# A transformer layer on one core: a two-half buffer for the sums of the values, and ranks counted in one work array

## The chip, the cores and the metric

The kernel runs on one core of a Trainium2 chip. The metric is the device time of one execution in microseconds (us). A core has five engines that run beside each other and meet at semaphores: PE (TensorE, matrix products), DVE (VectorE), ACT (ScalarE), POOL (GpSimd) and SP (SyncE, which here only issues DMAs).

## The reference

Eight sequences of 1,024 tokens with 256 channels go through one transformer layer. Cut to what matters:

```python
q, k, v = heads(ln(x) @ Wq + bq), heads(ln(x) @ Wk + bk), heads(ln(x) @ Wv + bv)   # 16 heads of 16
attn = softmax(where(causal, q @ k.T * scale, -inf))
x = x + ((attn * gate_of_each_key) @ v) @ Wo + bo
sc = sigmoid(ln(x) @ gate_w.T) + gate_bias           # 8 experts, 4 groups of 2
keep the 2 best groups, in them the 2 best experts (ties: the lower number first)
x = x + sum over the 2 experts of weight * ffn_e(ln(x)) + shared_ffn(ln(x))
```

## The kernel before

A batch is one of the eight sequences `n`. For each batch and each group `g` of four heads the kernel computes the running maxima of the scores (`M` on PE, `MR` on DVE, line 1549), then the scores (`QK` on PE, line 1941), their exponentials (`EX` on ACT, line 1358, into `probs`), the causal mask on the diagonal blocks (`MK` on POOL, line 1175), and the sums of the values (`PV` on PE, line 1961), which add up in one PSUM bank per half `c` of the queries (`CHUNKS` is 2, 512 queries each). When a half is summed, ACT copies the bank to SBUF (`OE`, `copy_o`, line 1369, into `o_sb`) and SP stores it to HBM (`SO`, `store_o`, line 978). That is 64 copies and 64 stores. `o_sb` is one buffer, so each copy waits on the semaphore `o_st` of the store before it, which belongs to the other half.

Behind the attention of batch `n` come its output product, the layer norm, the router's logits and the shared experts, quarter by quarter (`CW`, `CT`, `CG`, `EU`, `HT`, `ED`). The router then picks two experts for each token on DVE (`RO`, the function `routing`): `choose_op` ranks the four groups and then the eight experts with `rank_op`. A rank is the number of rivals that are greater, plus the number of equal rivals with a lower number. `rank_op` counts it in a cube of all pairs (128 partitions x 8 tiles x 8 x 8). For batches 0 to 6 it ranks all eight tiles of a batch at once (`ROUTE`), and the rows are scattered to their experts; for the last batch each quarter ranks its own two tiles (`DENSE_OPS` steps), and all eight experts are computed densely with the weights in `rank`, which line 1816 multiplies in.

No engine's order is written by hand. `plan_work` lists every piece of work with an engine, a planned duration, a due time, what it waits for and which PSUM bank it takes, and `Plan.run` lays them out in time; each engine then runs its pieces in the planned order. `LATER` is a table of offsets to the due times, one per kind of work. A change of one planned duration or one dependency can therefore move any later piece of work on any engine. Where the plan leaves PE idle for 500 ns or more while a sum is open, `keep_busy` puts in matmuls of zeros (line 858).

Of the kernel before, what the change touches and what calls it, by code (L numbers as in the profile page):

```python
# [79 lines left out]
RANK_OP = 13  # L80
# [20 lines left out]
DENSE_OPS = 19  # L101
# [227 lines left out]
def plan_work():  # L329
# [107 lines left out]
    def attention(n, g, s):  # L437
# [17 lines left out]
        if s in LAST_STEP:  # L455
# [3 lines left out]
                [("SO", (u - 1) // (GROUPS * CHUNKS), (u - 1) // CHUNKS % GROUPS, (u - 1) % CHUNKS)] if u else []),  # L459
# [70 lines left out]
    def routing(n):  # L530
        begin = at(n + 1) + T * SHARE_TO - 10000
        for r, step in enumerate(ROUTE[n]):
            ns = 620 if step in range(9, RANK_OP + 1) else 150
# [97 lines left out]
def build(nc, ins, out):  # L631
# [4 lines left out]
    with ExitStack() as ctx:  # L636
# [75 lines left out]
        o_sb = sb("o_sb", [P, CHUNK])  # L712
# [14 lines left out]
        cmp_b = sb("cmp_b", [P, TILES, EXPERTS, EXPERTS])  # L727
# [12 lines left out]
        slot_f = sb("slot_f", [P, 2, TILES])  # L740
        slot_u = sb("slot_u", [P, 4, 2, TILES], mybir.dt.uint32)
        owner, owner_old = sb("owner", [P, SLOT_TILES]), sb("owner_old", [P, SLOT_TILES])
        owner_i = sb("owner_i", [P, 2, SLOT_TILES], mybir.dt.int32)
        share = sb("share", [P, 2, TILES])
# [134 lines left out]
        def _(sp):  # L879
# [95 lines left out]
            def store_o(item, n, g, c):  # L975
                b, k = release["OE", n, g, c]
                sp.wait_ge(freed[b], k)
                sp.dma_start(o_s[bass.ds((n * GROUPS + g) * P, P), c * CHUNK:(c + 1) * CHUNK], o_sb[:]).then_inc(o_st[c], 16)
# [270 lines left out]
        def _(act):  # L1249
# [110 lines left out]
            def copy_o(item, n, g, c):  # L1360
# [104 lines left out]
        def _(dve):  # L1465
# [135 lines left out]
            def rank_op(r, v, n_v, to, ts):  # L1601
                a, b_ = cmp_a[:, ts, 0:n_v, 0:n_v], cmp_b[:, ts, 0:n_v, 0:n_v]
# [8 lines left out]
                if r == 2:  # L1611
                    return nc.vector.tensor_tensor(b_, other, mine, ALU.is_gt)
                if r == 3:
                    return nc.vector.tensor_tensor(a, a, b_, ALU.add)
                return nc.vector.tensor_reduce(to, a, X_AXIS, ALU.add)

            def choose_op(r, ts):
# [9 lines left out]
                if r < 8:  # L1627
                    return rank_op(r - 3, grp[:, ts, :], EXPERTS // 2, rank_g[:, ts, :], ts)
                if r == 8:
# [4 lines left out]
                return rank_op(r - 9, sel[:, ts, :], EXPERTS, rank[:, ts, :], ts)  # L1634
# [15 lines left out]
            def slot_op(n, step):  # L1650
# [58 lines left out]
                return nc.vector.tensor_copy(slot_u[:, n % 4, :, :], slot_f[:])  # L1709

            def owner_op(n, step):
# [10 lines left out]
                if step in ("owner_old", "owner"):  # L1722
                    return nc.vector.tensor_reduce((owner_old if step == "owner_old" else owner)[:], ends, X_AXIS, ALU.add)
                if step == "within":
                    return nc.vector.scalar_tensor_tensor(out=owner_old[:], in0=owner_old[:], scalar=float(EXPERTS),
# [419 lines left out]
```

## Time and profile before

| | |
|---|---|
| median of 3 executions | 1803.69 us (1797.37 to 1806.76) |
| the profiled execution's own time | 1808.59 us |
| its span, first to last instruction | 1806.6 us |
| mean granted TensorE clock | 0.962 of full |
| PE busy | 1653.0 us, 91% |
| DVE busy | 1292.4 us, 72% |
| ACT busy | 1081.9 us, 60% |
| POOL busy | 811.8 us, 45% |

The profile is of one execution, which was 4.9 us above the median. Busy shares are shares of the span. An instruction is named by its line in the kernel, its engine, its operation and output<-inputs.

### The profile page before, as it was taken

The numbers are of one execution on the slowest core, as the hardware profiler recorded it, in microseconds if no ns is written. First come the engines' busy times: TensorE is split into PE (matmuls) and PEld (weight loads), VectorE is DVE, ScalarE is ACT, GpSimd is POOL, SyncE is SP. The second block draws the span as 40 slices with busy tenths as digits, with TensorE's granted clock in tenths as the row PEclk, the third lists the DMA queues.
The fourth block names the chain that finished last, engine by engine and source line by source line (L and its number), as shares of the span: only waits on it lengthen the run. The fifth ranks groups of instructions, "written<-read, shape, count | busy, mean of one in ns | idle before, by whom it ended". The sixth has DMA issues, their size and how long they took to land.

```text
span 1806.6 us, 34673 instructions
## 1 busy us (share of the span) xinstructions
PE 1653.0 (91%) x12785; PEld 982.5 (54%) x12785; DVE 1292.4 (72%) x2528; ACT 1081.9 (60%) x1808; POOL 811.8 (45%) x1390
## 2 busy tenths in 40 slices
PE   7798989989988999899998989999999889999888
PEld 3344446435544566455654555555564557666677
DVE  5776767967795777777785757877688666963655
ACT  3466756665655655675656755586556765568432
POOL 5234533463345221632237863363207773157760
PEclk9699999999998999999998999999999999999999
DMA  5556655554445532644545665453535675336440
GB/s 151 158 156 194 176 169 152 182 153 124 125 127 147 158 104 87 174 113 120 159 118 151 185 194 152 127 162 108 147 93 172 198 197 159 97 129 199 135 122 13
DMA packets 192708, 261.25 MB, mean 145 GB/s; under 512 B 19616, under 2 KB 127264, under 8 KB 192544
## 3 DMA queue, kind: packets, MB, share of 16 engines
q1 hardware_dynamic: 181792, 229.67, 44.0%
q0 software_dynamic: 10752, 29.37, 5.6%
q8 instruction: 105, 1.72, 0.4%
q14 instruction: 59, 0.48, 0.1%
HBM read 130.98 MB, written 127.40 MB: 143 GB/s over the span
## 4 chain that ended last, share of the span: by engine, by line
PE 54%; DVE 14%; DMA 8%; ACT 8%; POOL 8%; issue 5%; SPq 3%; another core or an unknown queue 0%; POOLq 0%; ACTq 0%; DVEq 0%
PE ps_all L1961 10%; PE ps_all L2071 10%; DVE mx L1549 7%; PE ps_all L1941 6%; PE ps_all L1908 6%; PE ps_all L2102 5%; PE ps_all L1892 4%; ACT probs L1358 4%; PE ps_all L1878 3%; PE ps_all L1970 3%; POOL xs_s L1207 2%; PE ps_all L2081 2%; PE ps_all L2034 1%; DMA rr<-r_s 1%; DMA out<-rr 1%
## 5 line engine op out<-in xcount | busy, mean ns | idle before, releaser
L1549 DVE TENSOR_REDUCE mx<-ps_all 128x2 f32<-128x1024 f32 (+2 forms) x640 | 619.0, 1006 | 132.5 <-PE ps_all L1908 74.4
L1358 ACT ACTIVATE probs<-ps_all 128x1024 f32<-128x1024 f32 x576 | 571.8, 1028 | 218.0 <-PE ps_all L1941 209.9
L1175 POOL TENSOR_SCALAR_AFFINE_SELECT probs<-probs 128x256 f32<-128x256 f32 (+1 forms) x448 | 190.9, 443 | 495.5 <-ACT probs L1358 491.3
L1961 PE MATMUL ps_all<-probs,vaug 128*32 128x512 f32 (+3 forms) x3072 | 319.4, 516 | 21.9 <-POOL probs L1175 15.3
L1908 PE MATMUL ps_all<-k_st,q_st 63*128 63x512 f32 (+3 forms) x1536 | 269.3, 401 | 48.0 <-ACT probs L1358 16.3
L1941 PE MATMUL ps_all<-q_st,k_st 64*128 64x512 f32 (+3 forms) x1536 | 265.6, 401 | 29.3 <-ACT probs L1358 9.9
L1908 PEld LDWEIGHTS ps_all<-k_st,q_st 63*128 63x128 f32 x1536 | 135.1, 193 | 163.7 <-issue 52.2
L1941 PEld LDWEIGHTS ps_all<-q_st,k_st 64*128 64x128 f32 x1536 | 130.9, 191 | 158.9 <-issue 67.2
L2071 PE MATMUL ps_all<-w_hi,x2h 128*128 128x512 f32 (+1 forms) x480 | 168.2, 350 | 4.3 <-DVE x2l L1598 2.5
L1804 DVE SCALAR_TENSOR_TENSOR act_t<-act_t,ps_all 128x256 f32<-128x256 f32 x168 | 70.4, 419 | 123.4 <-ACT act_t L1421 110.9
L2071 PE MATMUL ps_all<-w_lo,x2h 128*128 128x512 f32 (+1 forms) x480 | 157.0, 327 | 0.0
L2071 PE MATMUL ps_all<-w_hi,x2l 128*128 128x512 f32 (+1 forms) x480 | 157.0, 327 | 0.0
L1421 ACT ACTIVATE act_t<-ps_all 128x256 f32<-128x256 f32 x168 | 64.6, 385 | 151.3 <-PE ps_all L2071 122.2
L1961 PEld LDWEIGHTS ps_all<-probs,vaug 128*32 128x32 f32 x3072 | 73.2, 110 | 131.6 <-issue 89.4
L1207 POOL DMA_INDIRECT xs_s<-xnb,slot_u x112 | 111.6, 996 | 42.9 <-issue 39.8
L1219 POOL DMA_INDIRECT yab<-ys_s,slot_u x112 | 108.3, 967 | 33.0 <-issue 20.2
L2102 PE MATMUL ps_all<-w_hi,h_hi 128*128 128x256 f32 (+1 forms) x336 | 109.5, 326 | 7.7 <-DVE h_lo L1831 6.9
L2071 PEld LDWEIGHTS ps_all<-w_hi,x2h 128*128 128x128 f32 x480 | 90.8, 189 | 27.6 <-issue 19.7
L1878 PE MATMUL ps_all<-wvd,xt 128*128 128x384 f32 x256 | 96.9, 506 | 1.8 <-issue 0.9
L2071 PEld LDWEIGHTS ps_all<-w_hi,x2l 128*128 128x128 f32 x480 | 90.9, 189 | 8.4
L1831 DVE TENSOR_TENSOR h_lo<-ps_all,h_hi 128x256 fp32r<-128x256 f32 x168 | 70.0, 419 | 35.1 <-ACT h_hi L1436 32.7
L2102 PE MATMUL ps_all<-w_lo,h_hi 128*128 128x256 f32 (+1 forms) x336 | 94.3, 281 | 0.0
(195 smaller groups left out, 2849.8 us busy)
## 6 DMA issues: line engine op xcount, KB each, us to landing
qk_s<-qh SPq DMA_DIRECT2D x116, 256.0 KB
q_st<-qk_s SPq DMA_DIRECT2D x128, 192.0 KB
k_st<-qk_s SPq DMA_DIRECT2D x128, 192.0 KB
xs<-xs_s SPq DMA_DIRECT2D x72, 256.0 KB
ys_s<-ysb SPq DMA_DIRECT2D x72, 256.0 KB
o_s<-o_sb SPq DMA_DIRECT2D x64, 256.0 KB
qk_s<-ql SPq DMA_DIRECT2D x57, 256.0 KB
xs_s<-ysb SPq DMA_DIRECT2D x20, 512.0 KB, 6.0
```

Of the source, the lines that this page charges most:

```text
L1175: last = nc.gpsimd.affine_select(out=block, in_=block, compare_op=ALU.is_ge, fill=0.0, base=0, pattern=[[0, heads], [1, P]], channel_multi ...
L1207: nc.gpsimd.indirect_dma_start(xs_s[i % 2], bass.IndirectOffsetOnAxis(ap=slot_u[:, n % 4, a, t:t + 1], axis=0), xnb[:, t, :], None).then_i ...
L1219: nc.gpsimd.indirect_dma_start(yab[:, t % 2, a, :], None, ys_s[SET_OF[n] % 2], bass.IndirectOffsetOnAxis(ap=slot_u[:, n % 4, a, t:t + 1], ...
L1358: nc.scalar.activation(to, of, ACT.Exp, scale=DH ** -0.5).then_inc(freed[release[item][0]], 1)
L1549: last = nc.vector.tensor_reduce(to[:, :, p, qt % QPC], both[:, :, at:at + keys], X_AXIS, ALU.max)
L1878: last = mm(bank(item)[:, 0:E + DP], xt[:, k, tt * P:(tt + 1) * P], wvd[:, k, :], start=(k == 0), stop=(k == KE - 1))
L1892: last = mm(bank(item), w[:, k, m * P:(m + 1) * P], xt[:, k, :], start=(k == 0), stop=(k == KE - 1))
L1908: last = mm(bank(item, j)[:, to:to + keys], q_st[r, q_half(n, g, c), p, qt % QPC * P:(qt % QPC + 1) * P], k_st[r, k_half(n, g, kc), p, 0:k ...
L1941: last = mm(bank(item, j)[:, to:to + cols], k_st[r, k_half(n, g, kt // QPC), a, kt % QPC * P:(kt % QPC + 1) * P], q_st[r, q_half(n, g, c), ...
L1961: last = mm(bank(first)[32 * h:32 * h + 32, q0 - c * CHUNK:], vaug[:, kt, g, h * VW:h * VW + 32], probs[:, s % 2, h, at:at + cols], start= ...
L2071: last = mm(bank(item)[:, to], x[:, buf, k, t * P:(t + 1) * P], w[:, k, cs], start=(k == 0 and j == 0), stop=(k == KE - 1 and j == 2))
L2102: last = mm(bank(first)[:, t * E:(t + 1) * E], h[:, z % 2, i * P:(i + 1) * P], w[:, cs], start=(item == first and i == 0 and j == 0), stop ...
```

## The change

`o_sb` gets a half for each half of the queries, and the copy of a half waits only for the store of the same half in the group before. In the plan the copy depends on the store two places back instead of one. `rank_op` counts the equal rivals in the work array `cmp_a` and reduces them, then counts the greater ones in the same array, reduces those into a small piece of `cmp_b`, and adds the two results; it had filled two arrays, added them and reduced once. It is six instructions instead of five, and it is called twice in a ranking, so `RANK_OP` and `DENSE_OPS` grow by two. In the plan one more step has the long duration (620) and one more the short one (150) in each ranking of batches 0 to 6. `cmp_b` shrinks from eight tiles to two; `slot_f`, `share` and `owner_old` become views of the work arrays.

```diff
-RANK_OP = 13
+RANK_OP = 15
-DENSE_OPS = 19
+DENSE_OPS = 21
...
             add("ACT", ("OE", n, g, c), 466, due + 4000, [("PV", n, g, s)] + (
-                [("SO", (u - 1) // (GROUPS * CHUNKS), (u - 1) // CHUNKS % GROUPS, (u - 1) % CHUNKS)] if u else []),
+                [("SO", (u - 2) // (GROUPS * CHUNKS), (u - 2) // CHUNKS % GROUPS, c)] if u >= CHUNKS else []),
                 frees=(first, None))
...
-            ns = 620 if step in range(9, RANK_OP + 1) else 150
+            ns = 620 if step in range(10, RANK_OP + 1) else 150
...
-        o_sb = sb("o_sb", [P, CHUNK])
+        o_sb = sb("o_sb", [P, CHUNKS, CHUNK])
...
-        cmp_b = sb("cmp_b", [P, TILES, EXPERTS, EXPERTS])
+        cmp_b = sb("cmp_b", [P, 2, EXPERTS, EXPERTS])
...
-                if c:
-                    act.wait_ge(o_st[0], (gi + 1) * 16)
-                else:
-                    act.wait_ge(o_st[1], gi * 16)
+                if gi:
+                    act.wait_ge(o_st[c], gi * 16)
                 first = FIRST_STEP[c]
-                nc.scalar.copy(o_sb[:], bank(("PV", n, g, first))).then_inc(freed[release[item][0]], 1)
+                nc.scalar.copy(o_sb[:, c, :], bank(("PV", n, g, first))).then_inc(freed[release[item][0]], 1)
...
-                a, b_ = cmp_a[:, ts, 0:n_v, 0:n_v], cmp_b[:, ts, 0:n_v, 0:n_v]
+                a, others = cmp_a[:, ts, 0:n_v, 0:n_v], cmp_b[:, 0, 0:ts.stop - ts.start, 0:n_v]
...
                 if r == 2:
-                    return nc.vector.tensor_tensor(b_, other, mine, ALU.is_gt)
+                    return nc.vector.tensor_reduce(to, a, X_AXIS, ALU.add)
                 if r == 3:
-                    return nc.vector.tensor_tensor(a, a, b_, ALU.add)
-                return nc.vector.tensor_reduce(to, a, X_AXIS, ALU.add)
+                    return nc.vector.tensor_tensor(a, other, mine, ALU.is_gt)
+                if r == 4:
+                    return nc.vector.tensor_reduce(others, a, X_AXIS, ALU.add)
+                return nc.vector.tensor_tensor(to, to, others, ALU.add)
```

The planned order differs in more places than these lines. On PE the orders are the same up to the scores (line 1941) that stand ahead of the place below, in the second batch's attention, and differ from there on: 6,213 rows before, 6,211 now. At that place stood, before:

```order
L1908 MATMUL ps_all<-k_st,q_st 128x512 x2
L1941 MATMUL ps_all<-q_st,k_st 128x512 x2
L858 MATMUL ps_all<-bars,scan 64x512
L1878 MATMUL ps_all<-wvd,xt 128x384 x2
L2102 MATMUL ps_all<-w_hi,h_hi 128x256
```

and now:

```order
L1908 MATMUL ps_all<-k_st,q_st 128x512 x2
L1941 MATMUL ps_all<-q_st,k_st 128x512 x2
L1878 MATMUL ps_all<-wvd,xt 128x384 x2
L2102 MATMUL ps_all<-w_hi,h_hi 128x256
L2102 MATMUL ps_all<-w_lo,h_hi 128x256
```

A matmul of zeros went; over the whole kernel there were 135 of them and there are 131. On ACT, in the same attention, the copy of the sums (`o_sb`) stood before:

```order
L1340 ACTIVATE rows_of<-ps_all 16x128
L1369 COPY o_sb<-ps_all 128x512
L1358 ACTIVATE probs<-ps_all 128x1024 x2
L1275 ACTIVATE qh<-ps_all,bqk 128x512
L1358 ACTIVATE probs<-ps_all 128x1024 x2
```

and stands now:

```order
L1340 ACTIVATE rows_of<-ps_all 16x128
L1275 ACTIVATE qh<-ps_all,bqk 128x512
L1358 ACTIVATE probs<-ps_all 128x1024 x2
L1367 COPY o_sb<-ps_all 128x512
L1358 ACTIVATE probs<-ps_all 128x1024 x2
```

The copy moved behind two exponentials and a copy of queries (`qh`). On DVE, in the last batch's third quarter, the ranking of the experts, with the work between its steps (`act_t` and `h_lo` are the dense experts), stood before:

```order
L1608 TENSOR_TENSOR cmp_a<-scan 128x128
L1820 SCALAR_TENSOR_TENSOR act_t<-act_t,ps_all 128x256
L1610 TENSOR_TENSOR cmp_a<-cmp_a,before 128x128
L1612 TENSOR_TENSOR cmp_b<-scan 128x128
L1614 TENSOR_TENSOR cmp_a<-cmp_a,cmp_b 128x128
L1615 TENSOR_REDUCE rank<-cmp_a 128x16
L1639 SCALAR_TENSOR_TENSOR rank<-rank,th 128x16
L1641 TENSOR_REDUCE den<-rank 128x2
L1804 SCALAR_TENSOR_TENSOR act_t<-act_t,ps_all 128x256
```

and stands now:

```order
L1820 SCALAR_TENSOR_TENSOR act_t<-act_t,ps_all 128x256
L1606 TENSOR_TENSOR cmp_a<-scan 128x128
L1608 TENSOR_TENSOR cmp_a<-cmp_a,before 128x128
L1610 TENSOR_REDUCE rank<-cmp_a 128x16
L1612 TENSOR_TENSOR cmp_a<-scan 128x128
L1614 TENSOR_REDUCE cmp_b<-cmp_a 128x16
L1615 TENSOR_TENSOR rank<-rank,cmp_b 128x16
L1804 SCALAR_TENSOR_TENSOR act_t<-act_t,ps_all 128x256
L1639 SCALAR_TENSOR_TENSOR rank<-rank,th 128x16
```

The add of two arrays became a reduce, one small add is new, and two steps of the dense experts moved ahead: line 1820 in front of the first step, and the next line 1804 in front of line 1639, where it had come behind line 1641.

## Rows read from the trace of the kernel before

**Rows 1.** The page: span, PE's busy time, and the shares of the last chain.

```profile
span 1806.6 us, 34673 instructions
PE 1653.0 (91%) x12785; PEld 982.5 (54%) x12785; DVE 1292.4 (72%) x2528; ACT 1081.9 (60%) x1808; POOL 811.8 (45%) x1390
...
PE 54%; DVE 14%; DMA 8%; ACT 8%; POOL 8%; issue 5%; SPq 3%; another core or an unknown queue 0%; POOLq 0%; ACTq 0%; DVEq 0%
```

**Rows 2.** Windows from one batch's last copy of sums to the next's, batches 2 to 7.

```profile
core 0: us, PE busy (x) PEld busy (x) DVE busy (x) ACT busy (x) POOL busy (x), PEclk, DMA share, GB/s
...
415.48:615.14 199.66, 184.08 (x1458) 101.04 (x1457) 150.72 (x287) 117.67 (x184) 78.82 (x140) 0.97 0.46 133
615.14:811.39 196.25, 184.49 (x1517) 110.35 (x1518) 149.48 (x283) 121.89 (x197) 71.91 (x130) 0.97 0.44 122
811.39:1029.37 217.98, 203.22 (x1604) 119.62 (x1603) 161.98 (x317) 134.66 (x226) 106.43 (x177) 0.96 0.51 145
1029.37:1235.18 205.81, 191.83 (x1512) 112.58 (x1514) 148.19 (x281) 131.90 (x220) 99.07 (x164) 0.98 0.53 152
1235.18:1453.84 218.66, 205.41 (x1662) 124.64 (x1664) 163.14 (x305) 139.15 (x234) 103.28 (x165) 0.99 0.52 151
1453.84:1673.11 219.27, 204.47 (x1713) 139.21 (x1714) 145.60 (x278) 143.87 (x261) 114.62 (x167) 0.98 0.53 156
```

**Rows 3.** The tile `o_sb`: the copies, their idle time before, who waited for them.

```profile
L1369 ACT COPY o_sb<-ps_all x64: 558/587/647, 81.4 to 1673.1; 128x512 f32<-128x512 f32 x64
...
  PE ps_all L1961: 39.2, 24
  issue: 0.6, 1
who waited for it (us, times):
  PEld ps_all L1961: 1.2, 4
...
  PE ps_all L1961: 0.2, 1
```

**Rows 4.** Timeline of ACT: the two copies of sums that stand closest, start and duration.

```profile
388.05 0.59 ACT L1369 COPY o_sb<-ps_all 128x512 f32<-128x512 f32 x1
...
396.29 0.59 ACT L1369 COPY o_sb<-ps_all 128x512 f32<-128x512 f32 x1
```

**Rows 5.** Groups of DVE by form: busy us, mean ns, idle time before.

```profile
L1669 DVE TENSOR_TENSOR scan<-scan 128x64 f32<-128x64 f32 x21 | 4.9, 233 | 0.3
L1614 DVE TENSOR_TENSOR cmp_a<-cmp_a,cmp_b 128x512 f32<-128x512 f32 x7 | 4.9, 697 | 0.0
...
L1615 DVE TENSOR_REDUCE rank<-cmp_a 128x64 f32<-128x512 f32 x7 | 4.7, 678 | 0.0
L1614 DVE TENSOR_TENSOR cmp_a<-cmp_a,cmp_b 128x128 f32<-128x128 f32 x11 | 4.6, 421 | 0.3
...
L1615 DVE TENSOR_REDUCE scan<-cmp_a 128x32 f32<-128x128 f32 x7 | 2.0, 282 | 0.0
```

**Rows 6.** Timeline of the third quarter's ranking in the last batch.

```profile
1753.90 0.50 DVE L1610 TENSOR_TENSOR cmp_a<-cmp_a,before 128x128 f32<-128x128 f32 x1
1754.44 1.26 DVE L1612 TENSOR_TENSOR cmp_b<-scan 128x128 f32<-128x128 f32 x1
1755.74 1.26 DVE L1614 TENSOR_TENSOR cmp_a<-cmp_a,cmp_b 128x128 f32<-128x128 f32 x1
...
1757.04 0.29 DVE L1615 TENSOR_REDUCE rank<-cmp_a 128x16 f32<-128x128 f32 x1
1757.36 0.17 DVE L1639 SCALAR_TENSOR_TENSOR rank<-rank,th 128x16 f32<-128x16 f32 x1
...
1754.22 1.34 POOL L1184 TENSOR_TENSOR oc<-oc,lb 128x512 f32<-128x512 f32 x1
1755.51 1.34 POOL L1185 TENSOR_TENSOR x<-x,bo 128x512 f32<-128x512 f32 x1
...
1759.53 0.44 PE L2081 MATMUL ps_all<-ident,act_t 128*128 128x128 f32 x2 [1.91 <-DVE act_t L1816]
```

**Rows 7.** PE groups by form: the matmuls of zeros.

```profile
L858 PE MATMUL ps_all<-bars,scan 128*64 128x512 bf16 x135 | 42.9, 408 | 0.0
```

More of the change, by code:

```diff
@@ L739, in build @@
             "count", "need", "room", "end", "row_old", "end_old", "jump"))
-        slot_f = sb("slot_f", [P, 2, TILES])
+        slot_f, share = cmp_a[:, TILES - 2, 0:2, :], cmp_a[:, TILES - 1, 0:2, :]
         slot_u = sb("slot_u", [P, 4, 2, TILES], mybir.dt.uint32)
-        owner, owner_old = sb("owner", [P, SLOT_TILES]), sb("owner_old", [P, SLOT_TILES])
+        owner = sb("owner", [P, SLOT_TILES])
+        owner_old = cmp_b[:, 0, :, :].rearrange("p a b -> p (a b)")[:, 0:SLOT_TILES]
         owner_i = sb("owner_i", [P, 2, SLOT_TILES], mybir.dt.int32)
-        share = sb("share", [P, 2, TILES])
         den = sb("den", [P, TILES])
@@ L977, in store_o @@
                 sp.wait_ge(freed[b], k)
-                sp.dma_start(o_s[bass.ds((n * GROUPS + g) * P, P), c * CHUNK:(c + 1) * CHUNK], o_sb[:]).then_inc(o_st[c], 16)
+                sp.dma_start(o_s[bass.ds((n * GROUPS + g) * P, P), c * CHUNK:(c + 1) * CHUNK], o_sb[:, c, :]).then_inc(o_st[c], 16)
             def load_l(item, n, c):
@@ L1626, in choose_op @@
                     return nc.vector.tensor_tensor(grp[:, ts, :], pairs[:, :, :, 0], pairs[:, :, :, 1], ALU.add)
-                if r < 8:
+                if r < 9:
                     return rank_op(r - 3, grp[:, ts, :], EXPERTS // 2, rank_g[:, ts, :], ts)
-                if r == 8:
+                if r == 9:
                     return nc.vector.scalar_tensor_tensor(
@@ L1708, in slot_op @@
                     return nc.vector.tensor_reduce(slot_f[:, int(step[-1]), :], tmp, X_AXIS, ALU.add)
-                return nc.vector.tensor_copy(slot_u[:, n % 4, :, :], slot_f[:])
+                return nc.vector.tensor_copy(slot_u[:, n % 4, :, :], slot_f)
             def owner_op(n, step):
@@ L1722, in owner_op @@
                 if step in ("owner_old", "owner"):
-                    return nc.vector.tensor_reduce((owner_old if step == "owner_old" else owner)[:], ends, X_AXIS, ALU.add)
+                    return nc.vector.tensor_reduce(owner_old if step == "owner_old" else owner[:], ends, X_AXIS, ALU.add)
                 if step == "within":
-                    return nc.vector.scalar_tensor_tensor(out=owner_old[:], in0=owner_old[:], scalar=float(EXPERTS),
-                                                          in1=owner_old[:], op0=ALU.is_lt, op1=ALU.mult)
+                    return nc.vector.scalar_tensor_tensor(out=owner_old, in0=owner_old, scalar=float(EXPERTS),
+                                                          in1=owner_old, op0=ALU.is_lt, op1=ALU.mult)
                 if step == "both":
-                    return nc.vector.tensor_tensor(owner[:], owner[:], owner_old[:], ALU.add)
+                    return nc.vector.tensor_tensor(owner[:], owner[:], owner_old, ALU.add)
                 return nc.vector.tensor_scalar(owner_i[:, SET_OF[n] % 2, :], owner[:], float(EXPERTS - 1), float(2 * F),
```

2 lines of the change are left out of this document (1 added, 1 removed).

## The prediction

> **What bounds the kernel now.** I read the page first. PE is busy for 1653.0 of 1806.6 us, and the chain that ended last is 54% PE, 14% DVE and 8% each of ACT, POOL and DMA [rows 1]. So PE is the bound, and the rest of the time lies in many short hand-offs. A busy DVE or ACT costs something only where PE waits for it.
>
> Then I read the windows [rows 2]. They are cut at the last copy of sums of each batch, so each holds one batch's attention and what runs beside it. Length less PE's busy time is PE's idle time: 15.58, 11.76, 14.76, 13.98, 13.25 and 14.80 us, 14.02 in the mean. DVE is busy for 66 to 76% of a window, ACT for 59 to 66%. PE's granted clock is between 0.96 and 0.99 of full, so PE runs at the upper of its two levels nearly all the time.
>
> Last I read the two things that the change names. The 64 copies of the sums had 39.2 us of idle time on ACT before them that PE ended, with line 1961, the sums themselves, and 0.6 us of issue [rows 3]. No DMA is in that list: no copy waited for the store before it. The two copies that stand closest begin 8.24 us apart, and one takes 0.59 us [rows 4], so even there the store had 7.65 us to land. The ranking takes DVE's time in short steps with no idle time of note before them [rows 5].
>
> **The change, part by part.**
>
> *The second half of the buffer.* The wait it takes away was never paid [rows 3], so its direct worth is 0. The bound on the other side is what others waited for the copies: seven entries between 1.2 and 0.2 us [rows 3], less than 7 x 1.2 = 8.4 us even if each were as long as the first. A copy can get earlier only in the planned order, and in the place shown it got later, behind two exponentials and a copy of queries. I take 0 and keep -8 to +1 for the range.
>
> *The ranking of batches 0 to 6.* For the groups, an add of two arrays (421 ns) goes; a reduce (282 ns) comes, and a small add of 128x32, which I bound from above by the 233 ns of the 128x64 form. For the experts, an add of 128x512 (697 ns) goes; a reduce (678 ns) and an add of 128x64 (233 ns) come [rows 5]. Together 282 + 233 + 678 + 233 - 421 - 697 = +308 ns per batch, and +2.2 us over seven. DVE has 24% or more of each window free [rows 2], which hides it. If that cover were gone the maxima behind it in DVE's queue would be late by 0.3 us per batch, and PE, which needs their PSUM banks, with them: +2.2 us at most. I take 0.
>
> *The last batch's four rankings.* Here little runs beside, and in the third quarter PE did wait for the weights: 1.91 us before line 2081 [rows 6]. Two more small instructions of about 0.2 us each lengthen that chain by 0.4 us. Against this stands what the rows show at the same place. Line 1612 and line 1614 took 1.26 us each, and ended at 1755.70 and 1757.00; POOL's lines 1184 and 1185 ran beside them and ended at 1755.56 and 1756.85. The reduce right behind, on an array of the same size, took 0.29 us [rows 6]. The DVE instruction seems to be held until the POOL instruction ends.
>
> The Trainium skill has a rule for this (GPSIMD Engine Reference, section 1, Specifications): the SBUF interfaces are shared with VectorE, with contention for DVE instructions that have two SBUF inputs. The trace agrees for these two; the rule would leave the new reduces free and would hold the two-input adds.
>
> I work the chain out both ways from the rows. If nothing is held, five steps become six and the chain grows by the small add: +0.2 us. If two-input instructions are held as in the rows, the equality count and its product are as before (to 1754.40), the reduce ends at 1754.73, the comparison is held to 1755.70, the second reduce ends at 1756.03, and the small add is held to 1757.00. Line 1639 then starts at 1757.04 and not at 1757.36: -0.3 us. The two answers differ by half a microsecond. For the group ranking ahead of it and for the other three quarters I add at most 0.4 us each. The sum over the last batch is +0.5 us, between -1 and +2.
>
> *The zeros.* 135 matmuls of zeros become 131, at 408 ns each [rows 7]. They fill planned idle time, so I take 0 for the four; if PE is never idle there it is -1.6 us.
>
> *The order.* This is the largest part. The planned durations and the one dependency move work on all five engines from the second batch's attention on. What the new order has to do is the same: the same products, copies, masks and transfers. What it changes is which hand-off has other PE work in front of it. I have no row for the new order, so I bound it by how much PE's idle time differs between stretches that do like work in differing local order, which is what the six windows are. Their idle times have a standard deviation of 1.4 us. For two independent orders over six batches that gives 1.4 x sqrt(12) = 5 us either way. The granted clock of the windows differs too, with a standard deviation of 0.01 [rows 2]; 1% of some 196 us of PE work is 2 us per batch, by the same rule 7 us at most. Together the order is worth 0, with a deviation of 8 or 9 us. Nothing in the two orders tells me the sign, so I take 0.
>
> *The sum.* 0 + 0 + 0.5 + 0 + 0 = +0.5 us. The profiled execution took 1808.59 us, of which 1806.6 are the span; the same execution would take 1809.1. It was 4.9 us above the median of the three, 1803.69, so my figure for the median is 1804.2, and I say 1804.
>
> **The rivals.** A measurement of this kernel can tell a change of about 0.5%, 9 us, from none.
>
> *The new order gives PE more idle time (slower).* The mechanism: DVE's queue now has the ranking's reduces and small adds between the reduces of the maxima, in another place of the attention; a maximum (line 1549) frees its pair of PSUM banks later, and the next matmuls of line 1908 or 1941 stand waiting. Its price: if each of the six whole batches comes to the idle time of the worst (15.58 for 14.02 us), 6 x 1.56 = 9.4 us, and some 2 us for the first and last stretches: 1815. It decides from 1.5 us a batch. For it: DVE is the second busiest engine and has 14% of the last chain [rows 1]. Against it: the ranking adds only 0.3 us a batch.
>
> *The new order gives PE less idle time (faster).* The same in the other direction: if each batch comes to the idle time of the best (11.76 us), 6 x 2.26 = 13.6 us, so 1790. For it: the copies of the sums no longer hold back a place in the plan. Against it: they never waited.
>
> *The copies come earlier and free their banks (a little faster).* The waits behind them, at most 8.4 us, shrink by half of that, so 1800. It lies within 0.5% and differs from the forecast only in the trace: the list of who waited for `o_sb` would be empty.
>
> *The change does not do what it says.* As for the wait on the store, that is my forecast itself: there was no wait to remove.
>
> **How the numbers follow.** The forecast, no change that can be told, 0.42; copies earlier, 0.06; slower by the order, 0.30; faster by the order, 0.22. The deviation of 8 or 9 us alone would put about 0.3 outside 9 us. I put 0.52 there, because one mistimed hand-off that repeats in each batch makes the batches move together, which the square root does not have. Slower gets more than faster since the ranking adds work and no row shows a wait that goes. So faster by over 0.5% 0.22, within 0.5% 0.48, slower by over 0.5% 0.30. The likeliest is 1804. The range takes in 1790 and 1815 and a few microseconds beyond: 1788 to 1821, with 0.1 left out on either side. The forecast's own range is 1795 to 1813.
>
> **What would show it.** In the profile of the changed kernel, the list of what ended the idle time before the copies should again hold PE and no DMA. The ranking's groups on DVE should have 22 more instructions and about 3 us more busy time, DVE in all 1295. PE's busy time should stay within 10 us of 1653; most of what the median moves by should be PE's idle time, spread over the batches and not in one place. In the last batch's third quarter the two reduces should take 0.3 us each even while POOL runs. I am wrong if a DMA ended copies' idle time before, unseen by the trace, which would show as a drop of more than 9 us with shorter gaps between PE's last sum and the copy; or if the new order holds one wait of more than 9 us that was not there, on a store, a load or a mask.

## The result and the profile after

| | before | after |
|---|---|---|
| median of 6 executions | 1800.89 us (1797.37 to 1806.76) | 1824.03 us (1821.34 to 1828.77) |
| the profiled execution's own time | 1808.59 us | 1828.77 us |
| mean granted TensorE clock | 0.962 | 0.956 |

The changed kernel takes 1.0133 of the time of before, 95% interval 1.0107 to 1.016: 23 us more. One execution of all those below, of d_new_order at 1858.39 us, fell in a slow state with a lower clock; it is in no ratio, and the median of that run's row is of its other five.

The page of the changed kernel, with the rows that answer to [rows 1]:

```profile
span 1827.0 us, 34675 instructions
PE 1661.0 (91%) x12781; PEld 989.1 (54%) x12781; DVE 1287.9 (70%) x2550; ACT 1081.1 (59%) x1808; POOL 811.0 (44%) x1390
...
PE 51%; DMA 12%; DVE 11%; POOL 8%; ACT 7%; SPq 5%; issue 5%; another core or an unknown queue 1%; POOLq 0%; DVEq 0%; ACTq 0%
```

The span grew by 20.4 us. Of this PE's busy time is 8.0 us (1661.0 less 1653.0), though four matmuls of zeros went, and its idle time is 12.4 us (166.0 less 153.6). The windows, cut at the last copy of each batch as in [rows 2], show where:

```profile
core 0: us, PE busy (x) PEld busy (x) DVE busy (x) ACT busy (x) POOL busy (x), PEclk, DMA share, GB/s
...
421.06:618.82 197.76, 183.40 (x1423) 100.46 (x1424) 147.39 (x283) 116.98 (x181) 79.16 (x140) 0.97 0.47 129
618.82:815.62 196.80, 184.04 (x1524) 110.18 (x1524) 149.22 (x281) 122.47 (x198) 70.80 (x130) 0.97 0.42 119
815.62:1041.49 225.87, 208.06 (x1611) 123.82 (x1611) 164.13 (x325) 138.88 (x235) 109.81 (x183) 0.96 0.53 154
1041.49:1246.26 204.77, 186.92 (x1518) 112.23 (x1517) 146.98 (x283) 127.99 (x214) 95.54 (x158) 0.98 0.50 144
1246.26:1474.56 228.30, 212.62 (x1703) 129.56 (x1704) 167.07 (x318) 141.34 (x239) 110.38 (x173) 0.98 0.54 153
1474.56:1700.03 225.47, 209.37 (x1681) 140.10 (x1679) 139.24 (x273) 141.06 (x255) 110.17 (x162) 0.95 0.48 144
```

Length less PE busy is 14.36, 12.76, 17.81, 17.85, 15.68 and 16.10 us. Against the six values of before that is -1.22, +1.00, +3.05, +3.87, +2.43 and +1.30, together +10.4 us. No batch has lost it all. Ahead of these windows PE's idle time grew by 6.4 us (56.8 of the first 421.06 us, for 50.5 of the first 415.48), and behind the last copy it fell by 4.4 us (14.6 of 126.97 us, for 19.0 of 133.49). The last window's granted clock is 0.95, where [rows 2] had 0.98.

The tile `o_sb`, as in [rows 3]:

```profile
L1367 ACT COPY o_sb<-ps_all x64: 558/586/621, 82.9 to 1700.0; 128x512 f32<-128x512 f32 x64
...
  PE ps_all L1961: 42.3, 23
  remote: 8.4, 2
  issue: 3.5, 3
who waited for it (us, times):
  PEld ps_all L1961: 2.3, 7
  PE ps_all L1908: 2.3, 1
```

Again no DMA stands among what the copies waited for. But there is an entry that [rows 3] did not have: `remote`, two waits of 8.4 us together. The word stands for a wait that ends on a semaphore's update although no instruction that raises this semaphore had ended in the 1.5 us before, by the record. The list of waits of the changed kernel has seven such rows (us in total, times, longest):

```profile
ACT probs L1358 <- remote: 15.2, 6, 6.6
ACT o_sb L1367 <- remote: 8.4, 2, 4.8
DVE mx L1547 <- remote: 5.2, 3, 3.6
ACT act_t L1419 <- remote: 5.0, 2, 3.8
DVE mx L1544 <- remote: 2.4, 1, 2.4
DVE vh L1496 <- remote: 1.6, 1, 1.6
ACT rows_of L1340 <- remote: 0.6, 1, 0.6
```

They sum to 38.4 us and are 16 waits, in 12 places (34.5 us where overlaps between engines are counted once). The same list of the kernel before has three rows:

```profile
ACT ysb L1448 <- remote: 2.4, 1, 2.4
DVE vh L1498 <- remote: 1.8, 1, 1.8
DVE mx L1549 <- remote: 1.7, 2, 1.5
```

That is 5.9 us. Every instruction in both lists reads a PSUM bank that PE wrote. I call these places late signals: PE's matmuls have ended by the record, and the reader starts some microseconds later.

The list shows only the worst of them. The trace holds the time of each semaphore update, and of the updates that PE's matmuls raise, 67 of some 2,400 came more than 0.6 us after the recorded end of the latest matmul that raises the same semaphore, with 123 us of delay in sum. In the trace of before it was 41, with 48 us. So the kernel before was not free of them either. No update of ACT, DVE or POOL came that late ahead of the last 5 us.

The ranking's groups on DVE stand now as follows, to be read against [rows 5]:

```profile
L1614 DVE TENSOR_REDUCE cmp_b<-cmp_a 128x64 f32<-128x512 f32 x7 | 4.8, 681 | 0.1
L1614 DVE TENSOR_REDUCE cmp_b<-cmp_a 128x32 f32<-128x128 f32 x7 | 2.0, 281 | 0.0
L1615 DVE TENSOR_TENSOR rank<-rank,cmp_b 128x64 f32<-128x64 f32 x7 | 1.6, 230 | 0.0
...
L1615 DVE TENSOR_TENSOR scan<-scan,cmp_b 128x32 f32<-128x32 f32 x7 | 1.3, 184 | 0.1
```

The added work per batch is 281 + 184 + 681 + 230 - 287 - 697 = +392 ns, where I had +308. The 287 is the mean of the add that goes (line 1614, 128x128) over the groups of batches 0 to 6. The 421 of [rows 5], with which I had worked, is the mean of eleven, and the four of them in the last batch took 656 ns in the mean: the longest was 1.27 us, one of those beside POOL in [rows 6].

### The profile page after: what moved, and what is told of

Read it like the earlier page. It is cut to its first block, busy times and chain, and to the rows that moved or that the text cites. A ratio compares the mean times of both kernels' runs of the same rounds, so it can differ in the third digit from the quotient of the medians.

```text
span 1827.0 us, 34675 instructions
## 1 busy us (share of the span) xinstructions
PE 1661.0 (91%) x12781; PEld 989.1 (54%) x12781; DVE 1287.9 (70%) x2550; ACT 1081.1 (59%) x1808; POOL 811.0 (44%) x1390
## 4 chain that ended last, share of the span: by engine, by line
PE 51%; DMA 12%; DVE 11%; POOL 8%; ACT 7%; SPq 5%; issue 5%; another core or an unknown queue 1%; POOLq 0%; DVEq 0%; ACTq 0%
PE ps_all L2071 10%; PE ps_all L1961 9%; PE ps_all L1908 6%; DVE mx L1547 6%; PE ps_all L2102 5%; PE ps_all L1941 5%; ACT probs L1358 4%; PE ps_all L1892 4%; PE ps_all L1878 3%; PE ps_all L1970 2%; POOL xs_s L1207 2%; PE ps_all L2081 2%; DMA qk_s<-ql 2%; DMA rr<-r_s 2%; DMA out<-rr 2%
## 5 line engine op out<-in xcount | busy, mean ns | idle before, releaser
L2071 PEld LDWEIGHTS ps_all<-w_lo,x2h 128*128 128x128 f32 x480 | 93.6, 195 | 4.9
```

The costliest lines, as they stand in the source:

```text
L2071: last = mm(bank(item)[:, to], x[:, buf, k, t * P:(t + 1) * P], w[:, k, cs], start=(k == 0 and j == 0), stop=(k == KE - 1 and j == 2))
```

## The experiments

Every kernel below ran beside the kernel before on the same chip. They were five chips; I call them A to E. The record does not name the chip of the first result, so it may be one of the five: B is like it in the time of before (1802.49 for 1800.89 us) and in its late signals. "Clean" means that no trace of that chip had a wait with no recorded releaser. Ratios are to the kernel before on the same chip, as recorded with their intervals; they are not quotients of the medians (i_after_160: 1802.69 over 1790.98 is 1.0065, the ratio 1.0097). A run has 4 to 10 executions, the kernel before 10 to 23.

| run | chip | median us | ratio | 95% | waits `remote`, us |
|---|---|---|---|---|---|
| b_ranks | A | 1798.92 | 1.0058 | 1.0035 to 1.0082 | 0 |
| c_old_order | A | 1790.67 | 1.0023 | 1.0000 to 1.0047 | 0 |
| d_new_order | A | 1796.67 | 1.0043 | 1.0012 to 1.0075 | 0 |
| a_dep | A | 1777.29 | 0.9934 | 0.9912 to 0.9957 | 0 |
| e_after_again | B | 1828.55 | 1.0142 | 1.0109 to 1.0176 | 23.9 |
| e_ranks_again | B | 1823.84 | 1.0114 | 1.0082 to 1.0146 | 32.6 |
| f_dep_order | B | 1805.45 | 1.0015 | 0.9991 to 1.0039 | 22.6 |
| g_order_160 | B | 1821.52 | 1.0093 | 1.0064 to 1.0122 | 14.9 |
| e_after_third | C | 1798.59 | 1.0053 | 1.0030 to 1.0075 | 0 |
| h_order_640 | C | 1806.61 | 1.0097 | 1.0069 to 1.0125 | 0 |
| i_after_160 | C | 1802.69 | 1.0097 | 1.0062 to 1.0133 | 0 |
| j_after_600 | C | 1796.04 | 1.0032 | 1.0009 to 1.0055 | 0 |
| l_order_oe | D | 1785.29 | 0.9959 | 0.9940 to 0.9978 | 0 |
| m_order_ex | D | 1798.26 | 1.0030 | 0.9999 to 1.0060 | 0 |
| n_order_cw | D | 1795.09 | 1.0009 | 0.9985 to 1.0033 | 0 |
| a_dep_again | D | 1781.26 | 0.9943 | 0.9919 to 0.9966 | 0 |
| e_after_fourth | E | 1798.61 | 1.0044 | 1.0027 to 1.0062 | 0 |
| o_no_scatter | E | 1751.02 | 0.9778 | 0.9749 to 0.9807 | 0 |

The kernel before had medians of 1789.12 us on A, 1802.49 on B, 1790.98 on C, 1793.02 on D and 1791.05 on E.

### First four: which part carries the loss

**b_ranks** is the changed kernel with the buffer's part undone; the ranking stays new.

```diff
-                [("SO", (u - 2) // (GROUPS * CHUNKS), (u - 2) // CHUNKS % GROUPS, c)] if u >= CHUNKS else []),
+                [("SO", (u - 1) // (GROUPS * CHUNKS), (u - 1) // CHUNKS % GROUPS, (u - 1) % CHUNKS)] if u else []),
...
-        o_sb = sb("o_sb", [P, CHUNKS, CHUNK])
+        o_sb = sb("o_sb", [P, CHUNK])
...
-                if gi:
-                    act.wait_ge(o_st[c], gi * 16)
+                if c:
+                    act.wait_ge(o_st[0], (gi + 1) * 16)
+                else:
+                    act.wait_ge(o_st[1], gi * 16)
```

> The changed kernel with the one-buffer o_sb back: its wait on the store of the other half, its dependency in the plan. The order of every engine comes out the same as the changed kernel's. If the order or the ranking costs the time, this takes as long as the changed kernel, 1824 us (1.013 of before). If the second half of the buffer costs it (its two copies that began late), this is back at 1801.

Its order came out the same as the changed kernel's on every engine. It measured 1.0058, which neither expectation had: 1.013 or 1.000. So the whole reordering of the changed kernel comes from the ranking's planned durations, and the second half of the buffer is not needed for the loss.

**c_old_order** has all of the change's instructions, in the order of the kernel before: the plan is made with the old constants and the old dependency, and each step of the ranking is then replaced by its new steps.

```diff
+NEW_OF = {**{r: [r] for r in range(7)}, 7: [7, 8], 8: [9], **{r: [r + 1] for r in range(9, 13)}, 13: [14, 15]}
...
+def plan_of_before():
...
+    RANK_OP, RANK_FROM, DENSE_OPS = 13, 9, 19
+    ROUTE = [route_steps(n) for n in range(B - 1)]
+    plan = plan_work()
...
-    plan = plan_work()
+    plan = plan_of_before()
```

> All instructions of the changed kernel, laid out in the order of the kernel before: on PE, ACT, POOL and SP not one row differs in its place; on DVE the ranking's added steps stand directly behind the step that they belong to. If the order costs the time: 1801 us, 0 to 3 us more for the 22 added DVE instructions. If the six-step ranking or the buffer costs it: 1820 or more.

It measured 1.0023, and the interval's lower end is 1.0000: the instructions and the buffer together cost 4.1 us of 1789, between 0 and 8.4.

**d_new_order** is the mirror image: the instructions of the kernel before, in the changed kernel's order, by the same means.

```diff
+OLD_OF = {**{r: [r] for r in range(8)}, 8: [], 9: [8], **{r: [r - 1] for r in range(10, 15)}, 15: []}
...
-    plan = plan_work()
+    plan = plan_of_after()
```

> All instructions of the kernel before (five-step ranking, one o_sb), laid out in the order of the changed kernel. If the order costs the time: 1820 to 1826 us, with nothing else changed. If the instructions cost it: 1801.

It measured 1.0043: the order alone costs 7.7 us, between 2.1 and 13.4. The direction is the first theory's, the size of 19 us or more is not. 4.1 + 7.7 = 11.8 us is 1.0066, which agrees with b_ranks; half of the first result's 1.0133 is not there on this chip.

**a_dep** is the kernel before with the one dependency of the plan changed. The buffer and its waits stay single.

```diff
-                [("SO", (u - 1) // (GROUPS * CHUNKS), (u - 1) // CHUNKS % GROUPS, (u - 1) % CHUNKS)] if u else []),
+                [("SO", (u - 2) // (GROUPS * CHUNKS), (u - 2) // CHUNKS % GROUPS, c)] if u >= CHUNKS else []),
```

> The kernel before with only the plan's dependency of the copy on the store two back; five-step ranking, one o_sb whose wait stays. The orders agree with before up to the fourth batch's attention and differ behind it. If any other order than that of before is worse (before's is a lucky one): slower by some 5 to 20 us. If the loss belongs to the one order that the ranking's planned durations give: within 5 us of 1801.

It measured 0.9934, faster than both kernels, which neither expectation had. It has the planned order that the buffer would have given alone. Its page:

```profile
span 1775.5 us, 34705 instructions
PE 1644.3 (93%) x12796; PEld 980.0 (55%) x12796; DVE 1286.5 (72%) x2528; ACT 1081.2 (61%) x1808; POOL 810.9 (46%) x1390
```

PE is idle for 131.2 us. The kernel before has no kept profile on this chip; c_old_order, which has its order, was idle for 146.0 us here. The gain is not the buffer's, since there is still only one: it is an order that happens to be better.

### Second four: the missing half of the loss

**e_after_again** is the changed kernel as it is; **e_ranks_again** is b_ranks again, without an edit.

> The changed kernel again, with nothing edited, beside the next kernel on one chip. With its order alone, the kernel before took 1.004 of its time, and with order and ranking 1.006, both on another chip than the first result (1.013). If the two-half buffer costs the rest in this order: 1.012 to 1.015 again, with waits before the copies of sums that the profile puts down to nothing on the core. If the chip or the moment made the first result larger: 1.004 to 1.008, as the next kernel.

> The changed kernel with one o_sb buffer, as in the earlier run: 1.006 of before again by either theory. It is the partner for the run above on the same chip.

1.0142 and 1.0114: on chip B the large loss was back, without the buffer's part too, where I had expected 1.006 for the second. The two intervals overlap. Now the same kernel could be compared at one place on two chips. In the sixth batch's attention the timeline of b_ranks on chip A has:

```profile
1371.63 1.50 PE L1963 MATMUL ps_all<-probs,vaug 128*32 128x384 f32 x24
...
1373.06 0.50 PE L1910 MATMUL ps_all<-k_st,q_st 63*128 63x512 f32 x2
1373.20 0.59 ACT L1369 COPY o_sb<-ps_all 128x512 f32<-128x512 f32 x1 [1.20 <-PE ps_all L1963]
```

The copy begins 0.07 us after the sums end (1373.13). The timeline of e_ranks_again on chip B, same place:

```profile
1367.91 1.50 PE L1963 MATMUL ps_all<-probs,vaug 128*32 128x384 f32 x24
...
1372.05 0.58 ACT L1369 COPY o_sb<-ps_all 128x512 f32<-128x512 f32 x1 [3.77 <-remote]
1372.09 1.23 DVE L1549 TENSOR_REDUCE mx<-ps_all 128x2 f32<-128x1024 f32 x1 [0.90 <-remote]
...
1372.78 0.51 PE L1910 MATMUL ps_all<-k_st,q_st 63*128 63x512 f32 x2 [2.46 <-ACT o_sb L1369]
```

Here the sums end at 1369.41 by the record and the copy begins 2.64 us later. At the same moment DVE's reduce of another bank gets going too, so it is not ACT that was late. PE then waits 2.46 us for the bank.

The profile models the end of a matmul, so a late end would look the same; the updates' own times speak for a late signal. The updates of these sums, of line 1910 behind them and of the two products of line 1943 behind that stand at 1372.03, 1372.07, 1372.11 and 1372.16, which is 2.6, 2.2, 2.0 and 1.8 us after their recorded ends, though line 1910 had started at 1369.35 and line 1943 at 1369.69. On chip A the same four came 0.02 to 0.04 us after the ends. So on B four updates of three semaphores came out in one burst, some 0.04 us apart. A second place in the same run:

```profile
1596.64 0.50 PE L1943 MATMUL ps_all<-q_st,k_st 64*128 64x512 f32 x2
...
1601.73 1.02 ACT L1358 ACTIVATE probs<-ps_all 128x1024 f32<-128x1024 f32 x1 [5.16 <-remote]
1602.81 0.79 PE L1910 MATMUL ps_all<-k_st,q_st 63*128 63x512 f32 x2 [5.66 <-ACT probs L1358]
...
1603.91 0.41 PE L2073 MATMUL ps_all<-w_lo,x2h 128*128 x1
```

The scores of 1596.64 are read at 1601.73, PE stands for 5.66 us, and its next matmuls of line 2073 take 0.41 us, where those ahead of the stall took 0.28. The granted clock was 0.50 of full, the lower level, from 1602.80 to 1606.00, and 0.99 in the 3 us after that. So such a place costs its wait and some of PE's speed behind it.

**f_dep_order** has all of the change's instructions in the order of a_dep (the kernel c_old_order with the new dependency in the plan).

> The changed kernel's instructions in the order that the new dependency of the copy gives without the ranking's new planned durations. If the ranking's planned durations spoil the order, and the work itself costs next to nothing: 0.993 to 0.997 of before, as the order alone gave 0.993 and the ranking and buffer in the old order cost 1.002. If the two-half buffer costs: 1.00 or more.

1.0015, on a chip with late signals, where the changed kernel had 1.0142: same instructions, same buffer, 23 us less, by the order alone. Its ratio is above the 0.993 to 0.997 that I had expected; on a chip with late signals it can't be told whether the buffer or they took the difference.

**g_order_160** is the kernel before with another number in the plan, to see how much any other order is worth:

```diff
-            ns = 620 if step in range(9, RANK_OP + 1) else 150
+            ns = 620 if step in range(9, RANK_OP + 1) else 160
```

> The kernel before, instructions untouched, with the planned duration of the short ranking steps at 160 for 150: the order differs from the same place of the second batch on as in the changed kernel. If orders simply scatter about by some 0.5%: anywhere between 0.990 and 1.010. If a longer planned ranking is what makes an order slow: 1.004 or more.

1.0093: 10 ns in the plan of short steps, and no new work, lose as much as the change's order or more. Both expectations allow that.

### Third four: the order on a clean chip

**e_after_third** is the changed kernel as it is. **h_order_640** is the kernel before with 640 for 620. **i_after_160** and **j_after_600** are the changed kernel with 160 for 150 and with 600 for 620 in the same line.

> The changed kernel once more, unedited, in the hope of another chip than the two on which it took 1.013 and 1.014. Two sizes are open: with its order and its ranking, but one buffer, 1.006 on a chip whose profile had no wait without a recorded releaser, 1.011 on one that had twelve. If such waits make up the difference: about 1.006 if this profile has none, 1.011 to 1.014 if it has some ten, 20 us or more in all. If the two-half buffer makes it: 1.010 or more with or without them.

> The kernel before, instructions untouched, with 640 for 620 as the planned duration of the long ranking steps: another order from the second batch on. Orders scatter: anywhere between 0.993 and 1.012. If a plan of a longer ranking is itself what makes orders slow: 1.004 or more, as with 160.

> The changed kernel, with 160 for 150 as the planned duration of the short ranking steps: the same instructions in another order from the third batch on. Orders scatter: 0.995 to 1.014. If the changed instructions cost the time whatever the order: 1.010 or more.

> The changed kernel, with 600 for 620 as the planned duration of the long ranking steps. Orders scatter: 0.995 to 1.014. If the changed instructions cost the time: 1.010 or more. A time of before or less would be a version of the change that does not lose.

The changed kernel measured 1.0053 here, and its list of waits had no `remote` row. Its page:

```profile
span 1794.9 us, 34675 instructions
PE 1645.6 (92%) x12781; PEld 981.2 (55%) x12781; DVE 1287.8 (72%) x2550; ACT 1081.1 (60%) x1808; POOL 812.2 (45%) x1390
```

Against the profile of the first result this is the same program with 16.7 us less PE idle time (149.3 for 166.0) and 15.4 us less PE busy time. Not all of that is the change's: the kernel before was slower there too, 1800.89 for 1790.98 us here. The others gave 1.0097 (h), 1.0097 (i) and 1.0032 (j). So the kernel before with 640 for 620 lost as the theory of the longer planned ranking has it, and no version of the change was as fast as before.

### Fourth four: orders that have nothing to do with the ranking

The kernel before with 10 ns more planned for the copy of the sums (**l_order_oe**), the exponentials (**m_order_ex**) or the shared experts' matmuls (**n_order_cw**), and a_dep again.

```diff
-            add("ACT", ("OE", n, g, c), 466, due + 4000, [("PV", n, g, s)] + (
+            add("ACT", ("OE", n, g, c), 476, due + 4000, [("PV", n, g, s)] + (
```

```diff
-            add("ACT", ("EX", n, g, s, p), 905, due + p * 1200, [("QK", n, g, s, p)],
+            add("ACT", ("EX", n, g, s, p), 915, due + p * 1200, [("QK", n, g, s, p)],
```

```diff
-            add("PE", ("CW", n, q, i), 860, pre + 7000, [("CP", n, q)], 1, FULL)
+            add("PE", ("CW", n, q, i), 870, pre + 7000, [("CP", n, q)], 1, FULL)
```

> The kernel before, instructions untouched, with 476 for 466 as the planned duration of the copy of the sums. The order differs behind the fifth batch's attention on PE. If any order but the old one loses: 1.001 to 1.010. If orders scatter about the old one: 0.993 to 1.007. It has nothing to do with the ranking.

> The kernel before, instructions untouched, with 915 for 905 as the planned duration of an exponential. The order differs from the first batch on. If any order but the old one loses: 1.003 to 1.012, as with the ranking's planned durations. If only a longer planned ranking makes an order slow: 0.993 to 1.003.

> The kernel before, instructions untouched, with 870 for 860 as the planned duration of the output product. The order differs from the second batch on. If any order but the old one loses: 1.003 to 1.012. If only a longer planned ranking makes an order slow: 0.993 to 1.003.

> The kernel before with only the plan's new dependency of the copy, again: it took 0.993 of before on a chip whose profiles had no wait without a recorded releaser. 0.990 to 0.997 again there; on a chip that has such waits it may come out up to 0.006 higher, as the changed kernel's order did.

0.9959, 1.0030 and 1.0009: within 0.5% of the old order, on either side of it. a_dep came out at 0.9943, so its gain is real. The six other orders for the old instructions on clean chips (d, h, l, m, n and a_dep, with the mean of its two runs) are +0.43, +0.97, -0.41, +0.30, +0.09 and -0.62% from the old one. Their mean is +0.13% and their standard deviation 0.58%, 10 us.

They are not plainly one scatter. The two whose plan has a longer ranking (d and h) are the two highest, and g_order_160, on chip B, is with them at +0.93%; the four whose plan leaves the ranking alone (l, m, n and a_dep) lie between -0.62 and +0.30%, as the expectation "if only a longer planned ranking makes an order slow: 0.993 to 1.003" has it. The versions of the change with that planned ranking (the change itself, b, i and j) are all above 1.003 as well. So the runs lean towards this rival over mere scatter. Seven orders do not settle it, and the run that would test it, the kernel before with a shorter planned ranking, was not made.

### Last two: are POOL's indirect DMAs behind the late signals?

All 12 places of the first result's trace lie where POOL issues the router's indirect DMAs (the scatter, line 1207, or the gather, line 1219). In ten one of them was running, and the other two began less than 0.5 us behind one. The stretches with these DMAs (gaps up to 2.5 us counted in) make up 368 of 1827 us, so chance alone would put 20% of the places there. The updates' times say the same of more places: in the six traces with late signals 348 of PE's updates are over 0.6 us late, and every one lies in such a stretch or within 2.4 us behind it, which is 27% of the time; in the 14 traces of the clean chips, no update is that late. All of those but o_no_scatter have the same 224 indirect DMAs, so the DMAs alone do not make updates late. **o_no_scatter** leaves them out: the routed experts then work on cleared rows, and their part of the result is missing. **e_after_fourth** is the changed kernel as it is, on the same chip.

```diff
-                nc.gpsimd.indirect_dma_start(
-                    xs_s[i % 2], bass.IndirectOffsetOnAxis(ap=slot_u[:, n % 4, a, t:t + 1], axis=0), xnb[:, t, :], None
-                    ).then_inc(xs_st, 16)
+                nc.gpsimd.memset(idle[:, col:col + 1], 0.0).then_inc(xs_st, 16)
...
-                    nc.gpsimd.indirect_dma_start(
-                        yab[:, t % 2, a, :], None, ys_s[SET_OF[n] % 2], bass.IndirectOffsetOnAxis(ap=slot_u[:, n % 4, a, t:t + 1], axis=0)
-                        ).then_inc(y_ld[t % 2], 16)
+                    nc.gpsimd.memset(yab[:, t % 2, a, :], 0.0).then_inc(y_ld[t % 2], 16)
```

> The changed kernel once more, as the control for the next run. If this chip is one of those on which signals come late, its trace has 6 to 12 places with waits that end with no recorded releaser, every one of them beside POOL's indirect DMAs (line 1207 or 1219) or within a few microseconds of them, and the ratio is 1.011 to 1.014. If it is one of the others, no such place and 1.003 to 1.008.

> The changed kernel without POOL's 224 indirect DMAs: a one-column fill stands in the place of each scatter and a fill of the same rows in the place of each gather, so the routed experts work on cleared rows and nothing of them reaches the output. All other work and every order stay. Theory 1, the late signals come from the indirect DMAs: no wait without a releaser is left, also where the control has 6 to 12, and the control's loss over its clean ratio (some 14 us) is saved beside what the DMAs themselves cost. Theory 2, the late signals have nothing to do with them and only stand there because the router's stretches hold much other work: some 4 to 12 places stay. If the control has none, this run says nothing on it, and gives only what the 224 DMAs cost: between 0 and 15 us, since POOL is busy for 44% of the span.

Chip E was clean: the control had no `remote` row, so the pair says nothing on the late signals, and the question stays open. The control gave the changed kernel a third clean ratio, 1.0044. And the 224 DMAs turned out to cost 1798.61 - 1751.02 = 47.6 us, three times the 15 us that I had put as their upper bound.

## Why the prediction was wrong

**The step that failed is the order's.** I took it as "worth 0, with a deviation of 8 or 9 us". On a clean chip d_new_order measured it at +7.7 us, and on the chip of the first result the whole change came to +23 us. The step holds two separate errors of different kinds.

*The sign, on a clean chip.* The changed kernel was at 1.0053 and 1.0044 and b_ranks, in the same order, at 1.0058: 1.0052 in the mean. On the 1803.69 us shown that is 1813 us. It is inside my range and 2 us from the rival "the new order gives PE more idle time", 1815. The size came near: six windows' idle times and clocks gave 8 to 9 us, six real orders gave 10. That is partly luck, since the windows differ in their work too, and the six orders may be two groups and not one scatter. Nothing that I had read told me that this order falls on the slow side; if a longer planned ranking makes orders slow, the sign stood in the plan's numbers, and I had no run to read it from. Of those 9 us, d_new_order puts 7.7 on the order.

*The late signals.* By the ratios they are the larger part of the miss, and nothing in my sum stood for them. This is argued from the difference between chips: no run took them away on a chip that has them. 1.0133 over 1.0052 is 1.0081, or 0.0081 x 1801 = 14.6 us on the chip of the first result; chip B has 1.0142 over 1.0052. On the chip of the first result the waits with no releaser grew from 5.9 us in the kernel before to 38.4 in the changed one, and PE's late updates from 41 to 67. The rows were in the trace of before, three of them, and I passed over them as small. The waits of this kind did not grow in proportion to the ratio: f_dep_order had 22.6 us of them and still only 1.0015. The number of late updates goes with it better: 46 there, 51 in g_order_160, 71 and 72 in e_after_again and e_ranks_again. What a late signal costs depends on what stands behind it, and that again is the order.

**Point by point.**

- *The buffer's wait was never paid, so its half is worth 0:* right. No DMA ended a copy's idle time, before or after. With and without the second half the clean ratios are 1.0053 and 1.0044 against 1.0058, and 1.0142 against 1.0114 on chip B, with overlapping intervals.
- *The ranking of batches 0 to 6, +308 ns each, hidden:* the size was +392 ns, 2.7 us over seven batches and not 2.2; I had taken the 421 ns of eleven adds for one of batches 0 to 6, where it was 287. Whether it is wholly hidden the runs can't tell: c_old_order gives 4.1 us for all instructions of the change, with 0.5 us, my figure, inside its interval of 0 to 8.4.
- *The last batch +0.5 us, between -1 and +2:* behind the last copy of sums the span was 6.5 us shorter and PE's idle time 4.4 us less. Line 2081 in the third quarter waited 0.44 us for the weights, where it had waited 1.91. d_new_order, with the old instructions, is as short there (126.3 us), so this is the order's doing, and my term left out that the order changes in this batch too.
- *DVE's busy time 1295 us:* wrong. It fell to 1287.9 with 22 more instructions. Over the runs of both sets of instructions it ranged from 1283.9 to 1293.5 us. How often POOL holds an instruction differs with the order, as the next point shows, and that alone can be more than the 3 us that I added; I did not trace the difference group by group.
- *Two-input instructions are held by POOL and the reduces are not:* right, as the third quarter of the last batch shows in the timeline of the changed kernel:

```profile
1776.48 1.34 POOL L1184 TENSOR_TENSOR oc<-oc,lb 128x512 f32<-128x512 f32 x1
1776.70 1.27 DVE L1608 TENSOR_TENSOR cmp_a<-cmp_a,before 128x128 f32<-128x128 f32 x1
1777.78 1.35 POOL L1185 TENSOR_TENSOR x<-x,bo 128x512 f32<-128x512 f32 x1
1778.01 0.29 DVE L1610 TENSOR_REDUCE rank<-cmp_a 128x16 f32<-128x128 f32 x1
1778.33 0.95 DVE L1612 TENSOR_TENSOR cmp_a<-scan 128x128 f32<-128x128 f32 x1
1779.31 0.29 DVE L1614 TENSOR_REDUCE cmp_b<-cmp_a 128x16 f32<-128x128 f32 x1
```

  Line 1608 ends at 1777.97, 0.15 us after POOL's line 1184 (1777.82). Line 1612 ends at 1779.28, 0.15 us after POOL's line 1185 (1779.13). The reduce between them takes 0.29 us in the middle of line 1185, as it did in [rows 6]. The rule of the Trainium skill (GPSIMD Engine Reference, section 1, Specifications) names DVE instructions in a 2-port perf mode or with two SBUF inputs. This trace agrees for lines 1608 and 1612, which have two, and for the reduce, which has one. The small add (line 1615) was not held, as I had it in the second way: it took 0.17 us at 1779.63, when line 1185 had ended.
- *PE's busy time within 10 us of 1653, and the loss spread over the batches:* right (1661.0; none of the six windows over +3.9 us of idle time). That most of the loss would be idle time holds for 12.4 of 20.4 us; the rest is PE's busy time, at a granted clock of 0.956 for 0.962.
- *The rival's mechanism, maxima that free their banks late:* not shown. DVE's share of the last chain fell from 14 to 11%, and DMA's grew from 8 to 12%. Its price, 1815, is near the clean chips' 1813, but its place is not established, so that is luck.
- *Copies earlier:* no. Others waited 5.4 us for them (the four entries of the tile's view, two of them under 0.6 us), and 3.8 us in the seven entries before.

**What stays open.** Why this order is slower than the old one on a clean chip; whether a longer planned ranking is behind it; and what makes the signals late. They were on the chip of the first result and on B, which may be the same chip, and in the first result, e_after_again and e_ranks_again mostly at the same places of the program, those of the first result all by POOL's indirect DMAs. None was in any of the 14 traces of the other four chips. The pair that would have told met a clean chip. That the DMAs are the cause is an inference from their place, not shown.

## What to carry to other kernels

Where a planner lays out the work, a change has two effects that must be measured apart: run its instructions in the old order, and the old instructions in its order. Any edit of a planned number draws a new order, here with a deviation of 0.58% or 10 us, so a small change is judged only in its own order's noise, and it pays to draw several orders: the kernel before with one dependency changed, 0.993 and 0.994 on two chips, beats both kernels, and the full change in that order came to 1.0015 where it had 1.0142. Measure on more than one chip, and read the waits that nothing in the trace explains before the result, however small they are.

## What the runs showed of the hardware that was not expected

- On chip B and in the first result the changed kernel had waits for PE of up to 6.6 us with no releaser in the record, at 6 and at 12 places; on C and E the same program had none, and on A b_ranks, in the same order, had none. The ratio to the kernel before went with it: 1.004 to 1.006 without, 1.011 to 1.014 with.
- There 41 to 72 of PE's semaphore updates per trace came more than 0.6 us late, some in bursts (four within 0.13 us, after up to 2.6 us): all in or within 2.4 us behind POOL's indirect DMAs; none of some 2,500 in each of 14 other traces.
- Behind a stall of 5.66 us, matmuls that had taken 0.28 us took 0.41, at a granted clock of 0.50.
- Leaving out 224 indirect DMAs of some 131 KB each, with POOL only 45% busy, saved 47.6 us. On chip E PE's busy time with them was 1645.8 us and without them 1632.8, and its idle time 151.1 and 118.2; the mean granted clock was 0.965 and 0.975. How much of that is their own time and how much the wait of the routed experts for their rows was not measured apart.
- A DVE instruction of two 128x128 inputs took 1.27 us beside POOL's 128x512 add of 1.34 us, and ended 0.15 us after it. The mean over the eleven instructions of its line and shape was 0.47 us.
